# Two cross-attentions over a 6272-key context: a new share of tiles turned on TensorE, later masks and weights, shared channel bounds

## The chip, the core and the metric

The kernel runs on one core of a Trainium2 chip. A core has TensorE (matmuls, here PE), VectorE (DVE), ScalarE (ACT), GpSimd (POOL) and SyncE (SP), which here only issues DMAs. The metric is the time of one execution on the device in microseconds (us), the median of several runs.

## What is computed

Two layers of a small Perceiver work on 64 tokens of width 128. Each layer is a cross-attention over a context of 6272 keys, a second block (self-attention; in layer 1 a delta-rule block) and a feed-forward block. This text is about the two cross-attentions. Attention 0 has a mask over the keys, attention 1 has none.

```python
x = x + _L0_xattn_ref(_layernorm(x, axis=-1), ctx_1024, mask_SxS2_ik0, W_q, W_k, W_v, W_o)
...
x = x + _L1_xattn_ref(_layernorm(x, axis=-1), ctx_1024, Wq, Wk, Wv, Wo, bo)
# each: 16 heads of 64; softmax(q k^T / 8, masked to -1e20 in the first) v, then W_o
```

The kernel never forms keys and values. It folds W_k into the queries (the tile G, 128 channels by 1024 rows, a row for each head and token), takes scores as G times the transposed context, and multiplies the probabilities with the untransposed context. Each float32 operand is kept as two float16 parts, upper and lower, and three of their four products are summed.

## The kernel before

**Tiling.** The keys are cut into 7 chunks of 896 (CH, CK), the 1024 rows into 8 tiles of 128 (RT). An attention has STEPS = 56 steps, n = 8 c + r. Each step passes through every engine:

- TensorE: `score(n)`, six matmuls (L443); two steps ahead of everything else.
- VectorE: `maximum(n)` (L556) applies scale and mask, writes `probs` and the running maximum; `shifted` (L561).
- ScalarE: `exps(n)`: `alpha` (L499, one column) and the exponential of the tile (L502).
- Either by DMA: ScalarE makes the upper half in float16 (`upper`, L509), VectorE or GpSimd subtracts it (`lower`, L532), SyncE issues one transposing DMA for both halves (`turn`, L392) into `probsT`.
- Or on TensorE: `turn(n)` is seven transposes into PSUM banks 4 and 5 (L455), ScalarE copies out the upper part (L516, L518), VectorE subtracts for the lower (L589). The next turn waits for `p_lower`, that is, for those banks.
- TensorE: `pv(n)`, 21 matmuls (L475), five steps behind; VectorE adds to `den` and `U` (L569, L574), six steps behind.

`on_pe(L, n)` says which steps are turned on TensorE, `on_vector(L, n)` which lower parts VectorE makes; the rest is GpSimd's. Every engine works through its list in order. `maximum(n)` also waits until the lower part of step n - 4 is done (`probs` has four buffers). `halves` has five buffers, `probsT` four.

**Context and masks.** SyncE's queue loads the context chunks first (float32, into `moe`), with mask 0 behind chunk 2 and masks 1 and 2 at the end; the others and the weights are in its list at fixed steps (`MASK_AT`, `WEIGHTS_AT`). In attention 0 GpSimd scales each chunk (L1119), casts its upper part (L1120), subtracts for the lower (L1124) and makes the bfloat16 mask (L1113), two steps apart, from step 0 on: chunk 2 + n // 6. A second transposing DMA per chunk (`turn_ctx`, L382) makes the untransposed context `ctxN`.

**Scales.** Before the first scores VectorE takes the largest absolute value of each channel in each chunk (`channel_max_dve`, L612, seven times) and derives the scale of the context. TensorE sums squares over the channels (L709) for a bound of the scores, GpSimd takes the root (L666), and VectorE and ScalarE write G's upper and lower halves (L756, L765, L788). In `fold_q_pe` the first half of G's matmuls (L714) is ahead of L709 and the second behind it. `stay_warm` (L686) issues matmuls whose result nobody reads.

## Time and profile before

| | us |
|---|---|
| median of 3 runs | 465.6 (462.07 to 466.75) |
| the profiled execution | 461.98 |
| its span | 460.2 |

| engine | busy us | share |
|---|---|---|
| TensorE matmuls | 414.4 | 90% |
| VectorE | 346.8 | 75% |
| ScalarE | 280.7 | 61% |
| GpSimd | 226.3 | 49% |

Attention 0 lies between about 26 and 181 us of the span, attention 1 between about 228 and 374 us. "L443" is a line of the kernel. In the page each group of instructions has its count, busy time, mean duration and the idle time of its engine before it, with what ended that idle time. A row of the timeline gives the start and duration of an instruction or of a merged row of equal ones. All times are of this one execution.

### The profile page before, as it was taken

What the parts mean: (1) busy time and instruction counts of PE and PEld (TensorE: products, weight loads), DVE (VectorE), ACT (ScalarE), POOL (GpSimd) and SP (SyncE); (2) the same over time, 40 slices, a digit from 0 to 9 for tenths busy, and PEclk for the clock granted to TensorE, in tenths of its full rate; (3) what the DMA queues carried; (4) which work ended last, traced back from release to release, by engine and by line L of the source; (5) the groups of instructions that cost most, each with busy time, mean ns of one, the idle gap of its engine ahead of it and who ended that gap; (6) DMA issues with size and microseconds to landing.
All of it is one profiled execution on the core that took longest, in us unless ns stands there. A gap on an engine that the chain in (4) does not pass through costs nothing.

```text
span 460.2 us, 11503 instructions
## 1 busy us (share of the span) xinstructions
PE 414.4 (90%) x4488; PEld 331.4 (72%) x4488; DVE 346.8 (75%) x939; ACT 280.7 (61%) x549; POOL 226.3 (49%) x143
## 2 busy tenths in 40 slices
PE   6897999999999998999888998999999899974776
PEld 6865777777877787889656776777777689853675
DVE  3676888888778887456599989888888854488653
ACT  2148788878888882433297897988898611260210
POOL 1379888798556540010014698875566100169110
PEclk8578999999999999999999999999999999995979
DMA  8738999999998889900049999999999910000000
GB/s 292 234 41 161 228 208 269 226 229 199 153 187 150 154 130 335 374 1 5 1 80 196 172 190 184 185 180 201 191 193 195 180 31 1 1 0 1 1 0 3
DMA packets 191365, 66.33 MB, mean 144 GB/s; under 512 B 186752, under 2 KB 186960, under 8 KB 190544
## 3 DMA queue, kind: packets, MB, share of 16 engines
q1 hardware_dynamic: 191024, 64.56, 71.9%
q10 hardware_dynamic: 288, 1.05, 0.6%
q8 instruction: 35, 0.57, 0.5%
q14 instruction: 18, 0.15, 0.1%
HBM read 18.76 MB, written 0.03 MB: 41 GB/s over the span
## 4 chain that ended last, share of the span: by engine, by line
PE 45%; DVE 21%; DMA 9%; POOL 9%; ACT 7%; issue 6%; SPq 3%; DVEq 0%; ACTq 0%; POOLq 0%
PE ps L475 15%; PE ps L443 12%; DVE probs L556 8%; DMA probsT<-halves 7%; PE ps L686 6%; ACT probs L502 3%; DMA moe<-in_ctxT 3%; POOL halves L532 2%; PE ps L455 2%; ACT halves L509 2%; POOL moe L1196 2%; PE ps L930 2%; DVE U L574 1%; POOL moe L1191 1%; SPq L392 1%
## 5 line engine op out<-in xcount | busy, mean ns | idle before, releaser
L532 POOL TENSOR_TENSOR halves<-probs,halves 128x896 f16<-128x896 f32 x70 | 132.3, 1891 | 88.5 <-ACT halves L509 87.9
L443 PE MATMUL ps<-ctxT_parts,GT_parts 128*128 128x512 f16 (+1 forms) x672 | 147.8, 357 | 10.0 <-DVE negmax L556 9.2
L475 PE MATMUL ps<-ctxN,probsT 128*128 128x128 f16 x2352 | 148.4, 219 | 5.5 <-DMA probsT<-halves 4.9
L475 PEld LDWEIGHTS ps<-ctxN,probsT 128*128 128x128 f16 x2352 | 139.0, 98 | 19.7 <-issue 5.5
L502 ACT ACTIVATE probs<-probs,shifted 128x896 f32<-128x896 f32 x112 | 115.3, 1030 | 0.0
L443 PEld LDWEIGHTS ps<-ctxT_parts,GT_parts 128*128 128x128 f16 x672 | 61.4, 99 | 62.6 <-DVE negmax L556 12.8
L509 ACT CAST halves<-probs 128x896 f16<-128x896 f32 x95 | 87.6, 922 | 0.0
L556 DVE CUSTOM_DVE_ANT_0 probs<-ps,maskb,negmax 128x896 f32<-128x896 f32 x56 | 67.5, 1205 | 3.7 <-PE ps L443 3.7
L556 DVE CUSTOM_DVE_ANT_0 probs<-ps,zero,negmax 128x896 f32<-128x896 f32 x56 | 67.5, 1205 | 0.5 <-PE ps L443 0.5
L686 PE MATMUL ps<-cst 128*128 128x128 f32 x458 | 65.4, 293 | 0.0
L686 PEld LDWEIGHTS ps<-cst 128*128 128x128 f32 x458 | 60.5, 206 | 3.3 <-issue 2.1
L499 ACT ACTIVATE alpha<-negmax 128x1 f32<-128x1 f32 x112 | 32.9, 294 | 48.3 <-DVE negmax L556 47.4
L574 DVE SCALAR_TENSOR_TENSOR U<-U,alpha,ps 128x128 f32<-128x128 f32 x112 | 38.4, 343 | 31.0 <-PE ps L475 30.5
L681 POOL TENSOR_TENSOR rstd<-veps,cst 128x1 f32<-128x1 f32 x6 | 3.3, 556 | 76.7 <-DVE veps L672 76.7
L532 DVE TENSOR_TENSOR halves<-probs,halves 128x896 f16<-128x896 f32 x25 | 30.2, 1210 | 1.5 <-ACT halves L509 1.5
L569 DVE TENSOR_SCALAR den<-den,alpha,chunksum 128x1 f32<-128x1 f32 x112 | 30.2, 269 | 0.1
L1113 POOL TENSOR_SCALAR maskb<-moe 128x896 bf16<-128x896 int32 x6 | 19.3, 3217 | 5.6 <-DMA moe<-in_mask 5.2
L502 ACT ACTIVATION_READ_ACCUMULATOR probs<-probs,shifted 128x1 f32 x112 | 20.9, 187 | 0.0
L589 DVE TENSOR_TENSOR probsT<-ps,probsT 128x512 f16<-128x512 f32 (+1 forms) x34 | 19.5, 615 | 1.1 <-ACT probsT L516 1.1
L561 DVE TENSOR_SCALAR shifted<-negmax 128x1 f32<-128x1 f32 x112 | 17.2, 154 | 3.9
L455 PE MATMUL ps<-cst,probs 128*128 128x128 f32 x119 | 16.6, 282 | 1.2 <-DVE probsT L589 1.2
L1532 DVE SCALAR_TENSOR_TENSOR moe<-ps,moe 128x63 f32<-128x63 f32 (+62 forms) x63 | 15.8, 251 | 2.2
(344 smaller groups left out, 390.7 us busy)
## 6 DMA issues: line engine op xcount, KB each, us to landing
moe<-in_ctxT SPq DMA_DIRECT2D x7, 448.0 KB, 9.5
moe<-in_mask SPq DMA_DIRECT2D x12, 224.0 KB, 6.4
moe<-in_gateT SPq DMA_DIRECT2D x2, 1024.0 KB, 9.4
moe<-in_upT SPq DMA_DIRECT2D x2, 1024.0 KB, 10.9
moe<-in_downT SPq DMA_DIRECT2D x2, 1024.0 KB, 13.4
probsT<-halves SPq DMA_TRANSPOSE x95, 4.7
wv<-in_wv SPq DMA_DIRECT2D x2, 512.0 KB, 5.9
wo<-in_wo SPq DMA_DIRECT2D x2, 512.0 KB, 6.9
```

The source lines that it names most:

```text
L443: ins = pe.matmul(ps[:, 2 * b + h, 0:width], GT_parts[:, g_part, r * P:(r + 1) * P], ctxT_parts[:, keys:keys + width], start=(g_part == 0 ...
L455: ins = pe.transpose(ps[:, TURN_BANKS[t // 4], t % 4 * P:(t % 4 + 1) * P], probs[:, n % BUFS, t * P:(t + 1) * P], ident)
L475: ins = pe.matmul(ps[:, bank, 0:D], probsT_parts[:, b, p_part, k * P:(k + 1) * P], ctxN_parts[:, at:at + D], start=(p_part == 0 and c_part ...
L499: act.activation(alpha[:, n:n + 1], negmax[:, n:n + 1], ACT.Exp, bias=negmax[:, n + RT:n + RT + 1], scale=-1.0)
L502: act.activation(probs[:, n % BUFS, :], probs[:, n % BUFS, :], ACT.Exp, bias=shifted[:, n:n + 1], scale=-1.0, accum_out=chunksum[:, n:n + ...
L509: act.copy(halves_of(L, n)[:, 0, :], probs[:, n % BUFS, :]).then_inc(sem("upper_done"), 1)
L532: eng.tensor_tensor(halves_of(L, n)[:, 1, :], probs[:, n % BUFS, :], halves_of(L, n)[:, 0, :], ALU.subtract).then_inc(lower_of(L, n)[0], 1)
L556: dve.tensor_tensor_reduce(out=probs[:, n % BUFS, :], in0=scored, in1=added, scale=descale[:, L:L + 1], scalar=negmax[:, n:n + 1], op0=ALU ...
L569: dve.tensor_scalar(den[:, r:r + 1], den[:, r:r + 1], alpha[:, n:n + 1], chunksum[:, n:n + 1], ALU.mult, ALU.add).then_inc(sem("den_added" ...
L574: dve.scalar_tensor_tensor(U[:, r, :], U[:, r, :], alpha[:, n:n + 1], ps[:, PV_BANKS[n % len(PV_BANKS)], 0:D], ALU.mult, ALU.add).then_inc ...
L589: dve.tensor_tensor(probsT_parts[:, n % BUFS, 1, a:a + w], ps[:, TURN_BANKS[part], 0:w], probsT_parts[:, n % BUFS, 0, a:a + w], ALU.subtra ...
L686: pe.matmul(ps[:, bank, 0:P], ident, ident, start=True, stop=True)
```

## The change

- Masks: all behind the context in SyncE's queue, the last five behind the first `turn_ctx`; `par` with them. GpSimd makes mask 0 after the root of the bound, mask 1 at step 2, and prepares chunks 2 to 6 from step 4 (`POOL_FROM`).
- Weights: at steps 24 to 44 instead of 12 to 22.
- Channel bounds: ScalarE takes chunks 1 and 4 as sums of absolute values (`channel_sum_act`), VectorE the other five.
- G of attention 0: the two parities alternate, all before L709, with eight warming matmuls between; 12 instead of 4 warming matmuls before the scores. ScalarE's half of G waits for the scale alone. In attention 1 the second lower half of G is made behind `maximum(0)`.
- Turning: in both attentions the steps n % 8 == 5 and the last three are turned on TensorE (9 + 9), where attention 0 had n % 4 == 3 and the last two (15), attention 1 the last two (2). The last two turns use banks 0, 1 and 2, 3 and wait for no lower part.
- Lower parts: VectorE makes those of 0, 2, then n % 4 == 3 up to 27, and 52 in attention 0. Upper and lower part of step 0 are one place earlier in the lists of ScalarE and VectorE.
- `alpha` of the first eight steps is a constant 0, so their L499 goes. The scale keeps an even exponent.

```diff
+POOL_FROM = 4
...
-        MASK_AT = {1: 3, 4: 4, 7: 5, 10: 6}
-        WEIGHTS_AT = {2: ("par", par[:], "par"), 12: ("in1", w_qT, "wqT1"), 13: ("in1", wkT[:], "wkT1"),
...
+        WEIGHTS_AT = {24: ("in1", w_qT, "wqT1"), 27: ("in1", wkT[:], "wkT1"), 30: ("out0", wv[:], "wv0"),
+                      33: ("out0", wo[:], "wo0"), 36: ("ffn", win[:], "win"), 38: ("ffn", wout[:], "wout"),
+                      40: ("small_attn", a_w[:], "a_w"), 42: ("delta", d_w[:], "d_w"), 44: ("delta", w1s[:], "w1s")}
         def on_pe(L, n):
-            return L == 0 and n % 4 == 3 or n >= STEPS - 2
+            return n % 8 == 5 or n >= STEPS - 3
         def on_vector(L, n):
             if L == 0:
-                return n < 30 and n % 4 == 1 or n == STEPS - 3
-            return n % 4 == 3 or n in (0, 1, STEPS - 3)
+                return n in (0, 2) or 4 <= n < 30 and n % 4 == 3 or n == STEPS - 4
+            return n % 4 == 3 or n in (0, 1, STEPS - 4)
+        def turn_banks(n):
+            return {STEPS - 2: (0, 1), STEPS - 1: (2, 3)}.get(n, TURN_BANKS)
...
-                if c == 2:
-                    load_mask(0)
+            load_mask(0)
             load_mask(1)
-            load_mask(2)
+            load("par", par[:], "par")
             turn_ctx(0)
+            for c in range(2, CH):
+                load_mask(c)
...
-                if k > 0:
+                if k > 0 and n < STEPS - 2:
                     pe.wait_ge(sem("p_lower"), 2 * k)
...
-                if 1 <= i <= STEPS and not on_pe(L, i - 1):
+                if i == 0:
+                    upper(0)
+                if 2 <= i <= STEPS and not on_pe(L, i - 1):
                     upper(i - 1)
...
-                if 2 <= i < STEPS + 2 and on_vector(L, i - 2) and not on_pe(L, i - 2):
+                if i == 1:
+                    lower(dve, L, 0)
+                if 3 <= i < STEPS + 2 and on_vector(L, i - 2) and not on_pe(L, i - 2):
                     lower(dve, L, i - 2)
...
+                for j in range(PAIRS):
+                    for par_ in range(2):
+                        rows = slice(par_ * DK, (par_ + 1) * DK)
+                        ins = pe.matmul(ps[:, 4 + par_, j * S:(j + 1) * S], wkT[rows, j, :], QT[rows, j, :],
+                                        start=True, stop=True)
+                ins.then_inc(sem("g_ready"), 2)
+                stay_warm(pe, 6, 8)
+                pe.wait_ge(sem("squares"), 2)
+                pe.matmul(ps[:, 7, 2 * D:2 * D + 3], C("ones"), squares[:, 0:3], start=True,
+                          stop=True).then_inc(sem("bound_summed"), 1)
+                return
...
-                channel_max_dve(dve, range(0, 3))
+                channel_max_dve(dve, (0, 2))
...
-                channel_max_dve(dve, range(3, CH))
+                channel_max_dve(dve, (3, 5, 6))
...
+        def channel_sum_act(act, c):
+            act.wait_ge(sem(f"ld_ctxT{c}"), 16)
+            act.activation(probs[:, c // 4, :], ctxT_raw[:, c * CK:(c + 1) * CK], ACT.Abs,
+                           accum_out=ch_amax[:, c:c + 1]).then_inc(sem("ch_max"), 1)
...
-            stay_warm(pe, 6, 4)
+            stay_warm(pe, 6, 12)
...
+            bound_pool(pool, 0)
             mask(0)
-            bound_pool(pool, 0)
...
-            mask(1)
             for n in range(STEPS):
                 if not on_pe(0, n) and not on_vector(0, n):
                     lower(pool, 0, n)
-                c, part = 2 + n // 6, n % 6
-                if c < CH:
+                if n == 2:
+                    mask(1)
+                c, part = 2 + (n - POOL_FROM) // 6, (n - POOL_FROM) % 6
+                if n >= POOL_FROM and c < CH:
...
-            flash_dve(dve, 1, {2: keep_o1, 4: partial(weight_max, 0, win), 6: partial(weight_max, 1, wout),
+            flash_dve(dve, 1, {0: partial(g_lower_dve, dve, 1, 1), 2: keep_o1, 4: partial(weight_max, 0, win), 6: partial(weight_max, 1, wout),
```

## Rows read from the trace of the kernel before

**Rows 1.** The page: the chain that ended last, shares by engine.
```profile
PE 45%; DVE 21%; DMA 9%; POOL 9%; ACT 7%; issue 6%; SPq 3%; DVEq 0%; ACTq 0%; POOLq 0%
```

**Rows 2.** By stretch: busy PE, PEld, DVE, ACT, POOL; clock, DMA share, GB/s.
```profile
44.00:110.00 66.00, 63.76 (x722) 48.74 (x720) 56.41 (x143) 53.24 (x105) 56.35 (x30) 1.00 1.15 228
110.00:168.00 58.00, 57.77 (x665) 45.25 (x663) 47.83 (x127) 49.01 (x98) 33.10 (x18) 1.00 0.95 165
168.00:182.00 14.00, 12.17 (x190) 11.47 (x187) 12.40 (x43) 5.87 (x13) 1.69 (x1) 1.00 0.95 239
228.00:254.00 26.00, 22.76 (x197) 15.20 (x195) 24.66 (x54) 20.38 (x39) 7.72 (x5) 1.00 0.70 124
275.00:305.00 30.00, 28.08 (x316) 20.42 (x314) 27.86 (x68) 24.98 (x48) 25.70 (x15) 1.00 1.11 176
```

**Rows 3.** Chain in order of time (start us, us, what), both attentions.
```profile
144.03 1.14 PE ps L443 x6
145.93 1.17 PE ps L475 x21
...
266.09 1.14 PE ps L443 x6
...
268.40 1.14 PE ps L443 x6
```

**Rows 4.** Chain before the first scores; last, the timeline at 187 us.
```profile
18.16 1.10 DVE ch_amax L612
...
20.85 3.60 PE ps L714 x16
24.45 2.00 PE ps L686 x8
26.46 2.25 PE ps L443 x6
...
187.26 2.06 PE L727 MATMUL ps<-wkT,wq 64*128 64x128 f32 x32
```

**Rows 5.** By stretch, 174:188; waits at 275:374 (us, times, longest); SyncE's queue, attention 1.
```profile
174.00:188.00 14.00, 12.44 (x178) 11.44 (x176) 9.00 (x32) 2.24 (x4) 0.00 (x0) 1.00 1.03 371
...
PE ps L475 <- DMA probsT<-halves: 3.7, 8, 1.1
...
235.28 132.57 SPq L392 DMA_TRANSPOSE probsT<-halves  x54
```

**Rows 6.** Timeline: start us, us, instruction; VectorE's subtraction beside GpSimd's work.
```profile
35.61 1.68 POOL L1119 TENSOR_TENSOR moe<-moe,ch_scale 128x896 f32<-128x896 f32 x1
...
35.76 2.48 DVE L532 TENSOR_TENSOR halves<-probs,halves 128x896 f16<-128x896 f32 x1 [1.20 <-ACT halves L509]
...
44.98 3.22 POOL L1113 TENSOR_SCALAR maskb<-moe 128x896 bf16<-128x896 int32 x1
...
47.55 1.08 DVE L532 TENSOR_TENSOR halves<-probs,halves 128x896 f16<-128x896 f32 x1
```

**Rows 7.** Timeline: GpSimd at steps 4 and 34, and the first product.
```profile
43.01 1.89 POOL L532 TENSOR_TENSOR halves<-probs,halves 128x896 f16<-128x896 f32 x1 [0.16 <-ACT halves L509]
...
44.59 1.33 PE L475 MATMUL ps<-ctxN,probsT 128*128 128x128 f16 x21
...
123.72 1.89 POOL L532 TENSOR_TENSOR halves<-probs,halves 128x896 f16<-128x896 f32 x1 [0.94 <-ACT halves L509]
```

**Rows 8.** GpSimd's groups at 44:110: busy us, mean ns; idle before, its end.
```profile
L532 POOL TENSOR_TENSOR halves<-probs,halves 128x896 f16<-128x896 f32 x13 | 24.6, 1891 | 9.1 <-ACT halves L509 8.8
...
L1124 POOL TENSOR_TENSOR ctxT_parts<-moe,ctxT_parts 128x896 f16<-128x896 f32 x4 | 7.6, 1892 | 0.0
...
L1120 POOL CAST ctxT_parts<-moe 128x896 f16<-128x896 f32 x4 | 5.3, 1337 | 0.3
```

**Rows 9.** Timeline of the last turn of attention 0; the page's group of L589.
```profile
175.63 0.95 PE L455 MATMUL ps<-cst,probs 128*128 128x128 f32 x7 [1.18 <-DVE probsT L589]
...
L589 DVE TENSOR_TENSOR probsT<-ps,probsT 128x512 f16<-128x512 f32 (+1 forms) x34 | 19.5, 615 | 1.1 <-ACT probsT L516 1.1
```

More of the change, by code:

```diff
@@ L50 @@
 HALF_SCALE = 2.0 ** 15
-CTX_SCALE = 2.0 ** 14
+CTX_SCALE = 2.0 ** 13
+EVEN_EXPONENT = 0x7F000000
 PROB_SCALE = 2.0 ** 11
@@ L411, in _ @@
                     load(name, t, src)
-                if n == 22:
-                    load("delta", w1s[:], "w1s")
             sp.wait_ge(sem("ctxT_ready"), CH)
@@ L497, in exps @@
             def exps(n):
-                act.wait_ge(sem("negmax_ready"), base + n + 1)
-                act.activation(alpha[:, n:n + 1], negmax[:, n:n + 1], ACT.Exp, bias=negmax[:, n + RT:n + RT + 1],
-                               scale=-1.0)
+                if n >= RT:
+                    act.wait_ge(sem("negmax_ready"), base + n + 1)
+                    act.activation(alpha[:, n:n + 1], negmax[:, n:n + 1], ACT.Exp,
+                                   bias=negmax[:, n + RT:n + RT + 1], scale=-1.0)
                 act.wait_ge(sem("shifted"), base + n + 1)
@@ L588, in turned_lower @@
                     dve.wait_ge(sem("p_upper"), 2 * pe_index(L, n) + part + 1)
-                    dve.tensor_tensor(probsT_parts[:, n % BUFS, 1, a:a + w], ps[:, TURN_BANKS[part], 0:w],
+                    dve.tensor_tensor(probsT_parts[:, n % BUFS, 1, a:a + w], ps[:, turn_banks(n)[part], 0:w],
                                       probsT_parts[:, n % BUFS, 0, a:a + w], ALU.subtract).then_inc(sem("p_lower"), 1)
@@ L620, in channel_scales_dve @@
             seq(dve.tensor_reduce(whole, ch_amax[:, 0:CH + 1], AX, ALU.max))
-            seq(dve.tensor_scalar(whole.bitcast(I32), whole.bitcast(I32), 0x7F800000, None, ALU.bitwise_and))
+            seq(dve.tensor_scalar(whole.bitcast(I32), whole.bitcast(I32), EVEN_EXPONENT, None, ALU.bitwise_and))
             dve.tensor_scalar(u_back[:], whole, 1.0 / CTX_SCALE, None, ALU.mult)
@@ L704, in fold_q_pe @@
                 pe.wait_ge(sem("q_copied"), 2)
-            for par_ in range(2):
-                rows = slice(par_ * DK, (par_ + 1) * DK)
-                if i == 0 and par_ == 1:
-                    pe.wait_ge(sem("squares"), 2)
-                    pe.matmul(ps[:, 7, 2 * D:2 * D + 3], C("ones"), squares[:, 0:3], start=True,
-                              stop=True).then_inc(sem("bound_summed"), 1)
-                for j in range(PAIRS):
-                    out = ps[:, 4 + par_, j * S:(j + 1) * S]
-                    if i == 0:
-                        ins = pe.matmul(out, wkT[rows, j, :], QT[rows, j, :], start=True, stop=True)
-                    else:
-                        for side in range(2):
-                            rows = slice(side * S, (side + 1) * S)
-                            ins = pe.matmul(ps[rows, 4 + par_, j * S:(j + 1) * S], w_qk[par_][:, j, rows], src[:, 0:S],
-                                            start=True, stop=True)
+                for j in range(PAIRS):
[9 more added lines that the diff above has]
+                return
+            for par_ in range(2):
+                for j in range(PAIRS):
+                    for side in range(2):
+                        rows = slice(side * S, (side + 1) * S)
+                        ins = pe.matmul(ps[rows, 4 + par_, j * S:(j + 1) * S], w_qk[par_][:, j, rows], src[:, 0:S],
+                                        start=True, stop=True)
                 ins.then_inc(sem("g_ready"), 1)
@@ L748, in fold_q_dve @@
                 ctxT_first_dve(dve, 0)
+                ctxT_first_dve(dve, 1)
             if i < 2:
@@ L757, in fold_q_dve, with g_lower_dve @@
                               ALU.mult).then_inc(sem("g_scaled"), 1)
+            dve.wait_ge(sem("g_scaled"), i + 1)
+            g_lower_dve(dve, i, 0)
+            descale_dve(dve, seq, i, kappa)
             if i == 0:
-                ctxT_first_dve(dve, 1)
-            dve.wait_ge(sem("g_scaled"), i + 1)
-            for half in range(2):
-                if half == 1:
-                    dve.wait_ge(sem("g_upper"), i + 1)
-                cols = slice(half * 4 * P, (half + 1) * 4 * P)
-                dve.scalar_tensor_tensor(GT_parts[:, 1, cols], ps[:, 4 + half, :], g_scale[:, i:i + 1],
-                                         GT_parts[:, 0, cols], ALU.mult, ALU.subtract).then_inc(sem("g_copied"), 1)
-            descale_dve(dve, seq, i, kappa)
+                g_lower_dve(dve, i, 1)
+        def g_lower_dve(dve, i, half):
+            if half == 1:
+                dve.wait_ge(sem("g_upper"), i + 1)
+            cols = slice(half * 4 * P, (half + 1) * 4 * P)
+            dve.scalar_tensor_tensor(GT_parts[:, 1, cols], ps[:, 4 + half, :], g_scale[:, i:i + 1],
+                                     GT_parts[:, 0, cols], ALU.mult, ALU.subtract).then_inc(sem("g_copied"), 1)
+        def channel_sum_act(act, c):
+            act.wait_ge(sem(f"ld_ctxT{c}"), 16)
+            act.activation(probs[:, c // 4, :], ctxT_raw[:, c * CK:(c + 1) * CK], ACT.Abs,
+                           accum_out=ch_amax[:, c:c + 1]).then_inc(sem("ch_max"), 1)
         def fold_q_act(act, i):
@@ L773, in fold_q_act @@
                                accum_out=squares[:, 0:1])
+                channel_sum_act(act, 1)
                 act.wait_ge(sem("q_ready"), 1)
@@ L1098, in pseq @@
                 pool.wait_ge(sem("pool_step"), steps[0])
+            pool.memset(alpha[:, 0:RT], 0.0)
             pool.memset(den[:], 0.0).then_inc(sem("cleared"), 1)
```

17 lines of the change are left out of this document (8 added, 9 removed).

## The prediction

> **What bounds the kernel now.** I read the chain of work that ended last, then busy time by stretch, then single steps. Both attentions run 56 steps of one shape: scores, maximum, exponential, a float16 upper part by ScalarE and the rest (lower part) by VectorE or GpSimd, the turn of the tile by a DMA or on TensorE, and the product with the context. Almost half of the chain is TensorE [rows 1]. In the second half of attention 0 TensorE is busy for 57.8 of 58 us [rows 2]. There a step is 1.14 us of scores and 1.17 us of product, 2.31 us. After a turned tile there is a hole of 0.76 us between the two (144.03 + 1.14 = 145.17, and the next product is at 145.93) [rows 3]. So a tile turned on TensorE costs it 0.76 us, and with every fourth tile turned a step costs 2.50 us. Attention 1, with two turned tiles in all, runs at 2.31 us a step where nothing else holds it (266.09 to 268.40) [rows 3]. With every eighth tile turned a step would cost 2.31 + 0.76/8 = 2.40 us.
>
> Other limits are close. At 44 to 110, the first half of attention 0, GpSimd is busy 56.4 of 66 us. VectorE is busy 24.7 of 26 us at the start of attention 1, and 27.9 of 30 at 275 to 305. TensorE is idle for 2.2 us at 44 to 110. The DMA share is 1.15 with masks and weights among the tiles, and 0.95 without [rows 2].
>
> **Attention 0, start.** The masks now come behind the context, so 448 KB less lies before the last context chunk, which is waited for until 18.16 [rows 4]. At 371 GB/s [rows 5] that is 1.2 us. Two of the seven channel bounds go to ScalarE, idle then. That saves at most the 1.1 us of one bound [rows 4]. Against it, TensorE must now finish all matmuls of G and eight warming ones before the matmul of the bound. One parity of G takes 3.6 us at the low clock. With the parities alternating, as in L727, 32 such matmuls took 2.06 us at full clock [rows 4]. At half the clock I estimate 3.7 to 4.1 us for all 32, about what one half took before. They then end at about 18.7 us. Warming at 0.25 us an instruction (8 took 2.00 [rows 4]) adds up to 4 us, so the bound is summed at 22.1 to 22.9, against 20.85. Behind it come the square root on GpSimd, the scale and the G tile, about 4 us, while 24 more warming instructions run. The first scores then start at about 27 us against 26.46. But six matmuls of scores took 2.25 us at the low clock [rows 4] and take 1.14 at the full one, so the first maximum starts 0 to 0.9 us sooner. If the clock stays low, the scores start at 28 us or later and it is 1 to 2 us later.
>
> Then the first lower part moves to VectorE, directly behind step 1, instead of waiting behind GpSimd's context work. The subtraction of step 1, which took VectorE 2.48 us [rows 6], goes to GpSimd. Walking through the queues with these durations I get the maximum of step 4 at about 35.5 us and the first product at about 42 us, against 44.59 [rows 7]. Gain 2.5 us, range 0 to 4. GpSimd, however, has the mask of chunk 1 (3.22 us [rows 6]) in between, and I find it at step 4's lower part at 43.3 us, against 43.01 [rows 7].
>
> **Attention 0, steps 4 to 33.** This is what I think decides. GpSimd prepares five chunks there, each 1.68 and 3.22 us [rows 6] and 1.34 and 1.89 us [rows 8], with gaps 8.3. Of the 30 steps TensorE turns four (5, 13, 21, 29) and VectorE subtracts six, so 20 lower parts of 1.89 us, with gaps 1.93, stay for GpSimd. That is 41.5 + 38.6 = 80.1 us of work, against 80.7 us in which the old kernel came from step 4 (43.01) to step 34 (123.72) [rows 7]. TensorE would like 30 x 2.40 = 72 us. So GpSimd becomes the bound, reaches step 34 when it did before, and the saved turns bring nothing in this stretch. Products still come earlier, because the subtraction had slack: 8.8 us of GpSimd's idle time was waiting for ScalarE [rows 8]. I keep 2.3 of the 2.5 us.
>
> One thing speaks against the change here. VectorE's subtraction took 2.48 us where GpSimd's product had begun just before it (35.61 to 37.29), 1.4 more than the 1.08 us it took inside GpSimd's mask operation [rows 6]. The Trainium skill, page SBUF — State Buffer, section SBUF: two separate sides, says that a VectorE operation with two inputs in SBUF and a GpSimd operation exclude each other for the whole instruction. The first pair of rows agrees with that, the second does not.
>
> **Attention 0, steps 34 to 52.** TensorE turns two tiles (37, 45) instead of five: -2.3 us. But the weights now load at steps 24 to 44. From step 24 to 43 the queue has 18 tiles and 3 context turns. The 54 transposes of attention 1 took 132.6 us from first to last issue [rows 5], 2.4 us each, and I take 2.35. That is 49.4 us, and 3.1 MB of weights at 371 GB/s are 8.4 us more: 57.8 us, for steps that TensorE does in 48. From the issue of step 24 at about 96 us it ends at 154 to 156 us, where the old kernel was too. Some hides in the DMA's lead over the product; I charge 1.3 us. Sum -1.0, between -2.3 and +2.
>
> **End of attention 0.** Three tiles are turned on TensorE, the last two into score banks that are free. Before, the last turn waited 1.18 us for VectorE [rows 9]. TensorE is idle for 1.8 us at 168 to 182 [rows 2]; one turn more costs 0.76: -1.1 us. Attention 0 in all: -2.3 - 1.0 - 1.1 = -4.4 us, range -10 to +2.
>
> **Attention 1.** The new order puts the lower part of step 0 between maximum 1 and 2 on VectorE, where it waits for ScalarE's cast. Queued behind that wait are maximum 2 and, for its result, ScalarE's next exponential and the cast of step 1. G's second half (L765) moves behind maximum 0. I get maximum 4 one us later. Through step 9 the turned tile of step 5 adds VectorE's two subtractions (2 x 0.615 us [rows 9]) and a later place for each maximum, where VectorE has nothing to spare: +3.0 us, range +1 to +3.5. Six more turns (13 to 53) at 0.76 us cost +4.6, since TensorE is the bound there. In return 3.7 us of waits for DMA go [rows 5], because a tile in eight leaves the queue, and the last turn's wait of 1.2 us: -4.9. Sum +2.7, range -2 to +7. Between and behind the attentions nothing changes that lies on the path; G's ScalarE half no longer waits for VectorE's, worth 0 to 0.4.
>
> **Sum.** -4.4 + 2.7 = -1.7 us. The profiled execution took 461.98 us with a span of 460.2, and lies 3.6 below the median of 465.6. I move the difference onto the median: 463.9, forecast 464.0 us.
>
> **Rivals.** (A) As summed: GpSimd and the queue take back what TensorE gives in attention 0, and attention 1 loses a little: 464.0, own range 461 to 469.
> (B) Faster: GpSimd does not hold the pace, since 9.1 us of its time at 44 to 110 was idle [rows 8] and steps can shift against each other. Then six turns fewer count in full, -4.6, the 2.2 us idle at 44 to 110 go, and with the start's 2.5 and the end's 1.8 attention 0 gives 11; attention 1 at +1 makes 455.6. Against it: 80 us of work in 72.
> (C) Slower: in attention 1 the DMA turns were hidden, and only 1.2 of the 4.9 us comes back. Then it is +3.0 + 4.6 - 1.2 = +6.4 there, and slower over all by more than 1% once attention 0 gives less than 1.7 us. With half of my 4.4 it is 469.8.
> (D) Slower: the two engines exclude each other. Each of the six VectorE subtractions costs GpSimd 1.08 us while it is the bound, +6.5: 470.4. The mask operation, which excluded nothing, speaks against the full price. This is the rule of the Trainium skill, page SBUF — State Buffer, section SBUF: two separate sides, taken at its word.
>
> **Chances.** A 0.42, B 0.36 (TensorE's pace is the one limit that is certain), C 0.12, D 0.10. One per cent, 4.7 us, is about what a measurement of this kernel can tell from no change. A lies within it, B on the fast side, C and D at or beyond the slow edge: faster 0.36, same 0.42, slower 0.22. The range takes in B, C and D: 455.5 to 470.5.
>
> **What would show it.** A: GpSimd busy over 90% from step 4 to step 34, its waits for ScalarE gone; B: still over 5 us of them, and steps of 2.40 us from the start. Steps 44 to 52 of attention 0 at 2.40 us. First product near 42 us. In attention 1 the first product one us later behind the first scores than now, waits for DMA under 1 us, steps of 2.40. Attention 0 shorter by 3 to 6 us, attention 1 longer by 1 to 4. The forecast would be wrong if attention 1 gets shorter, or if GpSimd idles at 44 to 110 us as it did.

## The result, and the profile after

| | before | after |
|---|---|---|
| median | 463.93 us (462.07 to 466.75) | 472.87 us (472.15 to 475.42) |
| ratio, 95% interval | | 1.0219 (1.0169 to 1.0269) |
| span of the profiled execution | 460.2 us | 470.5 us |

The changed kernel is 2.2% slower, where 464.0 us was forecast. The forecast was set on 465.6 us, the median of three executions; with the fourth it is 463.93, and taken from there the forecast change of -1.7 us gives 462.2. I cut both spans at the first matmul of scores and the end of the last product of each attention:

| us | first scores at | attention 0 | between | attention 1 | rest |
|---|---|---|---|---|---|
| before | 26.25 | 155.03 | 46.58 | 145.96 | 86.37 |
| after | 26.56 | 159.47 | 46.58 | 152.93 | 84.92 |
| difference | +0.3 | +4.4 | 0 | +7.0 | -1.5 |

The rest holds the same work in all kernels of this study, and varies between 84.9 and 87.9 us with the moments at which the granted clock is low. The loss lies in the attentions. The span came out 12.0 us above the forecast change; attention 0 accounts for 8.8 of them (-4.4 forecast, +4.4 measured) and attention 1 for 4.3 (+2.7 and +7.0).

Busy time by stretch, after (columns as in [rows 2]):

```profile
44.00:110.00 66.00, 61.27 (x699) 46.49 (x697) 56.58 (x136) 51.98 (x102) 64.01 (x33) 1.00 1.06 180
110.00:126.00 16.00, 11.83 (x107) 8.53 (x105) 8.28 (x22) 9.93 (x21) 15.55 (x9) 0.79 1.12 222
126.00:168.00 42.00, 40.74 (x472) 31.08 (x470) 32.56 (x86) 34.59 (x67) 26.47 (x14) 1.00 1.10 208
```

GpSimd is busy 64.0 of 66 us at 44 to 110, 97%, against 56.4 in [rows 2]: the forecast's first mark. But the loss is not there. It is in the second line: TensorE is busy 11.8 of 16 us and the mean of its granted clock is 0.79. This is the chain of work there, in order of time (start us, us, what):

```profile
104.56 3.94 POOL maskb L1136
...
108.58 1.89 POOL halves L537
110.48 1.64 POOL moe L1142
...
113.38 6.78 DMA probsT<-halves
120.16 0.14 issue
120.29 2.40 PE ps L477 x21
122.69 2.24 PE ps L445 x6
124.93 1.67 PE ps L477 x21
```

The product at 120.29 is that of step 28. Its turn was issued at 113.38 and took 6.8 us to land, against a median of 4.5 on the page. The chain goes from the turn back into GpSimd's list, and this is misleading. The lower part of step 28 is the one that began at 108.58, behind the mask, and it was ready at 110.47. The one that the chain puts before the turn began at 113.19, ended at 115.08 and is step 30's, so it can't have released a turn issued at 113.38. SyncE's queue (timeline) shows what held the turn for 2.9 us: three turns, the context turn of the next chunk and a 512 KB weight at its new place, issued almost without a pause:

```profile
102.65 7.40 SPq L397 DMA_TRANSPOSE probsT<-halves  x3
110.10 2.14 SPq L387 DMA_TRANSPOSE ctxN<-ctxT_parts  x1
112.28 0.58 SPq L366 DMA_DIRECT2D wkT<-in_wkT  x1
113.38 6.27 SPq L397 DMA_TRANSPOSE probsT<-halves  x2
```

The weight took 6.3 us to land. The product of step 28 waited 4.2 us, and everything behind it waited too: VectorE issues in order, so the addition of this product (L579) stood in front of the maximum of step 35 (L561). VectorE, timeline:

```profile
115.32 1.21 DVE L561 CUSTOM_DVE_ANT_0 probs<-ps,maskb,negmax 128x896 f32<-128x896 f32 x1
...
122.73 0.35 DVE L579 SCALAR_TENSOR_TENSOR U<-U,alpha,ps 128x128 f32<-128x128 f32 x1 [5.80 <-PE ps L477]
122.99 1.21 DVE L561 CUSTOM_DVE_ANT_0 probs<-ps,maskb,negmax 128x896 f32<-128x896 f32 x1
```

One late turn thus stops the scores, the exponentials and the next turns, and the lead is gone. TensorE paused from 116.1 to 120.29 us, and the granted clock was at its lower level (1.2 GHz) from 119.01 to 125.83. The 21 matmuls of the product took 2.40 us instead of 1.33, and the three groups from 120.29 on took 6.1 us, where 1.17, 1.14 and 1.17 us at the full clock make 3.5. So about 2.7 us of the loss at this place is the clock's. In all, products of attention 0 waited for DMA three times after 44 us, 7.3 us in sum, where it was 1.1 us in before. After:

```profile
PE ps L477 <- DMA probsT<-halves: 7.3, 3, 4.2
```

The table sets the starts of products against the first scores of the same attention, in us.

| product of step | 0 | 4 | 8 | 24 | 36 | 48 | 55 |
|---|---|---|---|---|---|---|---|
| attention 0, before | 18.35 | 28.34 | 38.74 | 81.45 | 111.83 | 141.81 | 153.69 |
| attention 0, after | 15.49 | 26.23 | 37.16 | 79.30 | 115.61 | 145.59 | 158.13 |
| attention 1, before | 14.09 | 24.91 | 34.59 | 73.82 | 102.79 | 131.80 | 144.62 |
| attention 1, after | 14.97 | 28.21 | 38.18 | 79.74 | 109.96 | 139.21 | 151.59 |

In attention 0, steps 24 to 36 take 36.3 us instead of 30.4: +5.9. In attention 1, 3.6 of the 7.0 us are lost by step 8 and 3.8 more from there to step 48, as much as five turned tiles of 0.76 us cost. The row of waits for DMA that stood in [rows 5] with 3.7 us has no counterpart in attention 1 after.

### The profile page after: what moved, and what is told of

Its sections match the earlier page's. It is cut to its first block, busy times and chain, and to the rows that moved or that the text cites. A ratio compares the mean times of both kernels' runs of the same rounds, so it can differ in the third digit from the quotient of the medians.

```text
span 470.5 us, 11565 instructions
## 1 busy us (share of the span) xinstructions
PE 415.5 (88%) x4527; PEld 332.3 (71%) x4527; DVE 347.5 (74%) x939; ACT 279.6 (59%) x538; POOL 225.7 (48%) x143
## 3 DMA queue, kind: packets, MB, share of 16 engines
q1 hardware_dynamic: 189200, 64.10, 69.7%
## 4 chain that ended last, share of the span: by engine, by line
PE 42%; DVE 20%; POOL 19%; issue 6%; ACT 6%; DMA 5%; SPq 1%; DVEq 0%; POOLq 0%; ACTq 0%
PE ps L477 13%; PE ps L445 10%; DVE probs L561 8%; POOL halves L537 7%; PE ps L695 6%; DMA probsT<-halves 4%; POOL maskb L1136 3%; ACT probs L505 2%; ACT halves L512 2%; PE ps L457 2%; POOL moe L1220 2%; PE ps L952 2%; POOL moe L1142 2%; POOL ctxT_parts L1147 1%; POOL moe L1215 1%
## 5 line engine op out<-in xcount | busy, mean ns | idle before, releaser
L537 POOL TENSOR_TENSOR halves<-probs,halves 128x896 f16<-128x896 f32 x69 | 130.2, 1891 | 92.2 <-ACT halves L512 91.2
L477 PE MATMUL ps<-ctxN,probsT 128*128 128x128 f16 x2352 | 151.0, 221 | 8.6 <-DMA probsT<-halves 7.3
L477 PEld LDWEIGHTS ps<-ctxN,probsT 128*128 128x128 f16 x2352 | 141.8, 99 | 22.2 <-issue 7.8
L561 DVE CUSTOM_DVE_ANT_0 probs<-ps,maskb,negmax 128x896 f32<-128x896 f32 x56 | 67.5, 1205 | 3.1 <-POOL halves L537 2.5
L561 DVE CUSTOM_DVE_ANT_0 probs<-ps,zero,negmax 128x896 f32<-128x896 f32 x56 | 67.5, 1205 | 1.9 <-PE ps L445 1.3
L695 PE MATMUL ps<-cst 128*128 128x128 f32 x490 | 67.8, 288 | 0.0
L695 PEld LDWEIGHTS ps<-cst 128*128 128x128 f32 x490 | 62.9, 202 | 3.3 <-issue 2.1
L579 DVE SCALAR_TENSOR_TENSOR U<-U,alpha,ps 128x128 f32<-128x128 f32 x112 | 38.3, 342 | 35.3 <-PE ps L477 34.7
L502 ACT ACTIVATE alpha<-negmax 128x1 f32<-128x1 f32 x96 | 28.2, 294 | 49.1 <-DVE negmax L561 48.4
L537 DVE TENSOR_TENSOR halves<-probs,halves 128x896 f16<-128x896 f32 x25 | 31.7, 1268 | 2.4 <-ACT halves L512 2.3
L594 DVE TENSOR_TENSOR probsT<-ps,probsT 128x512 f16<-128x512 f32 (+1 forms) x36 | 20.6, 615 | 2.8 <-ACT probsT L519 2.8
L1136 POOL TENSOR_SCALAR maskb<-moe 128x896 bf16<-128x896 int32 x6 | 20.8, 3471 | 0.5
## 6 DMA issues: line engine op xcount, KB each, us to landing
moe<-in_downT SPq DMA_DIRECT2D x2, 1024.0 KB, 12.8
```

The source lines that it names most:

```text
L477: ins = pe.matmul(ps[:, bank, 0:D], probsT_parts[:, b, p_part, k * P:(k + 1) * P], ctxN_parts[:, at:at + D], start=(p_part == 0 and c_part ...
L502: act.activation(alpha[:, n:n + 1], negmax[:, n:n + 1], ACT.Exp, bias=negmax[:, n + RT:n + RT + 1], scale=-1.0)
L537: eng.tensor_tensor(halves_of(L, n)[:, 1, :], probs[:, n % BUFS, :], halves_of(L, n)[:, 0, :], ALU.subtract).then_inc(lower_of(L, n)[0], 1)
L561: dve.tensor_tensor_reduce(out=probs[:, n % BUFS, :], in0=scored, in1=added, scale=descale[:, L:L + 1], scalar=negmax[:, n:n + 1], op0=ALU ...
L579: dve.scalar_tensor_tensor(U[:, r, :], U[:, r, :], alpha[:, n:n + 1], ps[:, PV_BANKS[n % len(PV_BANKS)], 0:D], ALU.mult, ALU.add).then_inc ...
L695: pe.matmul(ps[:, bank, 0:P], ident, ident, start=True, stop=True)
```

## Experiments

All lengths of attentions and steps below are of one profiled execution each. Two theories for attention 0. Q: SyncE's queue and DMA decide. Six tiles more go by DMA, weights stand among them, and a late turn stops everything. G, the forecast's mechanism: GpSimd decides. For attention 1 the question is whether the turned tiles do it.

### Move the weights earlier

```diff
-        WEIGHTS_AT = {24: ..., 27: ..., 30: ..., 33: ..., 36: ..., 38: ..., 40: ..., 42: ..., 44: ...}
+        WEIGHTS_AT = {12: ..., 13: ..., 15: ..., 16: ..., 18: ..., 19: ..., 21: ..., 22: ..., 23: ...}
```

> The changed kernel, with the weights loaded at steps 12 to 23 again instead of 24 to 44. Theory Q (the queue: in the changed kernel the transpose of step 28 landed at 120.16 us behind a 512 KB weight issued at 112.28, the product waited 4.2 us for it, VectorE's list stood behind the product and the clock was low until 125.8): without weights at steps 27 and 30 this stall goes, the changed kernel's 472.9 us fall by 3 to 6 us. Theory G (GpSimd is full from step 4 to 33, so lower parts and with them the transposes come late whatever else is in the queue): 0 to -1.5 us, a stall of similar size stays near step 28 to 35.

Measured: 469.15 us against 463.54, ratio 1.0136 (1.0068 to 1.0203), attention 0 157.65, 1.8 less than after. That is less than Q expected (3 to 6), and the wait of step 28's product shrank from 4.2 to 1.2 us, where G expected a stall of similar size. The stall moved with the weights. It opens at step 16, whose product waited 2.35 us, and steps 12 to 20 take 26.4 us instead of after's 21.1. Waits at 44 to 110 (us, times, longest):

```profile
PE ps L475 <- DMA probsT<-halves: 6.8, 6, 2.4
```

With every eighth tile on TensorE, the weights opened a stall in both places tried.

### Lighten GpSimd

```diff
+            pool.memset(maskb[:, 2 * CK:], 0.0)
...
             def mask(c):
+                w = CK if c < 2 else 8
-                pool.tensor_scalar(maskb[:, c * CK:(c + 1) * CK], mask_raw(c), 0.0, ...
+                pool.tensor_scalar(maskb[:, c * CK:c * CK + w], mask_raw(c)[:, 0:w], 0.0, ...
```

> The changed kernel, with GpSimd's mask operation for chunks 2 to 6 cut to 8 of 896 columns (the rest of the mask is zero, so most of the key mask of these chunks is left out of the computation). Takes 5 x 3.2 to 3.9 us of work from GpSimd between steps 8 and 32 and nothing else. Theory G: attention 0 returns towards TensorE's pace of 2.40 us a step and loses 6 to 10 us, GpSimd's waits for ScalarE grow by about 16 us. Theory Q: at most 2 us less, the wait of the product of step 28 for its transpose stays.

The masks of chunks 2 to 6 are then left out but for 8 columns each, so this kernel computes something else; it serves as a measurement of time alone.

Measured: 469.54 us against 463.54, ratio 1.0107 (1.0036 to 1.0177). The profiled execution is the slowest of four, with a span of 470.1; attention 0 is 160.95 us in it, against after's 159.47. GpSimd lost its load, the stall stayed:

```profile
44.00:110.00 66.00, 61.69 (x699) 46.49 (x698) 57.55 (x140) 54.59 (x108) 54.52 (x35) 1.00 1.06 186
110.00:126.00 16.00, 11.91 (x114) 8.63 (x112) 8.01 (x21) 8.74 (x17) 9.07 (x6) 0.79 1.10 214
```

GpSimd is busy 54.5 instead of 64.0 us and TensorE gains next to nothing (61.7 against 61.3); waits for DMA are 8.0 us. The chain of work at the stall:

```profile
102.72 1.90 POOL halves L537
...
106.59 2.08 SPq L387
...
108.72 0.58 SPq L366
...
109.82 6.66 DMA probsT<-halves
...
116.61 2.40 PE ps L477 x21
```

The lower part of step 28 was ready at 104.61 and its turn was issued at 109.82: it lay 5.2 us behind other turns, the context turn and the weight. With the weights where the change puts them, GpSimd's load is not what opens the stall. Against the first scores the product of step 36 came 0.8 us sooner than in after and that of step 48 0.3 us; from step 48 to 52, with the granted clock low from 175.97 to 179.38 us, it lost 1.8, and so its attention 0 is the longer one. G had expected 6 to 10 us. How much the relief gives in the median is less sure: two executions with a granted clock of 0.956 took 471.7 and 471.9 us, after at 0.960 to 0.964 took 472.2 to 475.4, and two at 0.98 took 466.5 and 467.4. Of those two there is no trace.

### More tiles on TensorE in attention 0

```diff
-            return n % 8 == 5 or n >= STEPS - 3
+            return n % 8 == 5 or L == 0 and n % 4 == 1 and n > 1 or n >= STEPS - 3
```

> The changed kernel, with n % 4 == 1 (5, 9, 13, ... 49) and the last three tiles of attention 0 turned on TensorE instead of n % 8 == 5; attention 1 as changed. Takes six lower parts of 1.9 us from GpSimd and six transposes from the queue, three of them before step 30, and adds six turns of 0.76 us to TensorE. Theory G or Q: attention 0 gets 3 to 6 us shorter. Theory T alone (TensorE's own work sets attention 0): 2 to 4.6 us longer.

Measured: 466.71 us, ratio 1.006 (1.0024 to 1.0096), attention 0 155.92, waits for DMA 1.2 us. Steps 24 to 36 take 31.8 us instead of 36.3. Turning six tiles on TensorE, which costs it 4.6 us, still makes attention 0 3.6 us shorter. The edit relieves the queue and GpSimd together and doesn't tell the two apart.

### Weights behind the last turn

```diff
-        WEIGHTS_AT = {24: ..., ..., 44: ...}
+        WEIGHTS_AT = {}
...
+            load("out0", ...); load("in1", ...); load("small_attn", ...)
             load_experts(0)
             load_experts(1)
+            load("ffn", ...); load("delta", ...)
```

> The changed kernel, but none of the nine weight loads stands among attention 0's steps: all are issued behind its last turn, in the order in which they are needed (the values' and output weights, the folded ones, the small attention's, then the experts, the feed-forward's and the delta branch's). Theory Q (the transfers of turned tiles, context turns and 512 KB weights share one queue, and a weight ahead of a turn is what opens the stall of steps 28 to 36): that stall goes, DMA waits of attention 0 fall from 7.3 us to about 1, attention 0 falls from 159.5 to about 155.5 us, and the span by about 4 us, if the later weights are still in time for the gap between the attentions; if the gap pays, it shows as more than 46.6 us between the last product of attention 0 and the first scores of attention 1. Rival (the queue is full by its turns alone, 1.2 turned tiles and context turns more per eight steps than before): the stall moves but stays, attention 0 at 158 to 160 us.

Measured: 466.21 us, ratio 1.0072 (1.0038 to 1.0106). Attention 0 is 155.35 us, -4.1, as theory Q says; the stretch between the attentions grew by 0.4 us. Without the weights in the queue, the turn of step 28 was issued 1.8 us earlier against the first scores, at 110.48, and still took 6.1 us to land. Its product waited 1.6 us instead of 4.2, and the clock didn't fall there: the 2.7 us that this had cost are part of the 4.1. But waits for DMA are 4.4 us, not 1: a second limit shows behind the first. The chain of work from 99.71 to 124.87 us lies on GpSimd almost throughout. GpSimd at steps 32 to 34, timeline:

```profile
117.66 1.91 POOL L544 TENSOR_TENSOR halves<-probs,halves 128x896 f16<-128x896 f32 x1
119.66 3.22 POOL L1143 TENSOR_SCALAR maskb<-UT 128x896 bf16<-128x896 int32 x1
122.95 3.73 POOL L544 TENSOR_TENSOR halves<-probs,halves 128x896 f16<-128x896 f32 x2
```

The last mask stands between two lower parts. ScalarE had cast the upper part of step 33 from 117.00 to 117.92; GpSimd began its lower part five microseconds later.

### Both

> The kernel weights_end, and with GpSimd's mask operation cut to 8 of 896 columns in chunks 2 to 6 (the rest of the key mask of these chunks is left out of the computation). GpSimd gets about 3 us less work per chunk, 15 us in all over steps 4 to 33. If GpSimd bounds steps 4 to 33 once the queue is free (the prediction's term), attention 0 falls by 2 to 5 us below weights_end; if it does not, the two differ by less than 1 us.

This kernel, too, leaves out most of the masks. Measured: attention 0 151.56 us, 3.8 less than weights_end (median 462.90 against 466.21 on the same chip). Steps 24 to 36 take 31.2 us against 33.8. Busy time by stretch:

```profile
44.00:110.00 66.00, 61.82 (x701) 46.75 (x700) 56.81 (x137) 52.48 (x102) 54.87 (x35) 1.00 1.03 178
110.00:126.00 16.00, 14.52 (x166) 10.78 (x165) 12.39 (x34) 13.45 (x27) 13.34 (x9) 1.00 1.11 187
```

TensorE is busy 14.5 of 16 us in the second stretch, 13.3 in weights_end and 11.9 in light_masks. So GpSimd does bound, worth 3.8 us, once the weights are out of the queue. While they are in it, the same relief gave under 1 us up to step 48. The 3.8 us come behind step 24: up to it the two kernels differ by 0.6 us.

### The eighth pattern in attention 0 alone

The kernel before with

```diff
-            return L == 0 and n % 4 == 3 or n >= STEPS - 2
+            return L == 0 and n % 8 == 5 or n >= STEPS - 2
...
-                return n < 30 and n % 4 == 1 or n == STEPS - 3
+                return n < 30 and n % 4 == 3 or n == STEPS - 3
```

> The kernel before with one part alone: in attention 0 TensorE turns the steps with n mod 8 = 5 and the last two instead of every fourth, so that seven tiles more go by DMA there (and VectorE's lower parts move from the steps with n mod 4 = 1 to those with n mod 4 = 3). Weights at 12 to 23. Theory Q: the six or seven more turns fill the queue, the weights of steps 12 to 23 then open a stall as in early_weights, DMA waits of attention 0 go from 1 to 6 to 10 us and attention 0 gets longer, to 157 to 160 us although TensorE saves 7 times 0.76 = 5.3 us of transposes; ratio 1.005 to 1.01. Rival (the prediction's: fewer turned tiles are worth 2.3 us or nothing, the queue costs 1.3): attention 0 at 153.5 to 155.5 us.

Measured: 469.50 us, ratio 1.0141 (1.0063 to 1.0218). Attention 0 is 162.76 us, +7.7, more than either theory said, although TensorE turns six tiles less:

```profile
PE ps L475 <- DMA probsT<-halves: 11.4, 8, 2.5
```

Before puts masks and weights among the turns of steps 1 to 22. Steps 4 to 8 take 12.1 us (before 10.4) and steps 12 to 20 25.9 us (before 21.9). The edit also gives GpSimd eight lower parts more (40 instead of 32). This is not what held the turns: at seven of the eight waits the lower part was ready 3.1 to 7.8 us before SyncE issued its turn (step 12: ready 67.61, issued 75.36).

### The late weights alone

The kernel before with WEIGHTS_AT at 24 to 44.

> The kernel before with one part of the change alone: the nine weights at steps 24 to 44 instead of 12 to 23. In before the queue has 14 tiles less of attention 0 to turn, and its DMA waits in attention 0 were 1.1 us. Theory Q in its full form (a weight hurts only a queue that the turns already fill): attention 0 stays at 155.0 us within 0.7, ratio 1.00. Rival (a late weight by itself, next to the context turn and an odd-numbered row of turns, opens the stall): attention 0 at 157 to 159 us.

Measured: 461.82 us, ratio 0.9996 (0.9953 to 1.0038): no change in the time. Attention 0 is 157.89 us in its profile, which is the rival's figure and not Q's. But by the product of step 8 it is already 1.9 us behind before, and up to step 12 the two have the same code. The product of step 5 had waited 2.1 us for its turn, and the clock was low behind that. At step 24 it is still 1.9 us behind, and from 24 to 52 it takes 69.7 us against 68.7. A late weight costs little where every fourth tile is turned on TensorE.

This run also shows how much one execution can differ from another of the same code. TensorE, timeline:

```profile
38.78 1.31 PE L439 MATMUL ps<-ctxT_parts,GT_parts 128*128 128x512 f16 x6 [2.70 <-DVE negmax L552]
39.93 0.93 PE L451 MATMUL ps<-cst,probs 128*128 128x128 f32 x7
...
42.27 1.33 PE L471 MATMUL ps<-ctxN,probsT 128*128 128x128 f16 x21
```

The first product comes 16.47 us after the first scores (at 25.81), in before 18.35. In before the granted clock was at the lower level from 39.62 to 43.03 us, and the same groups took 2.27 and 1.68 us:

```profile
39.43 2.27 PE L443 MATMUL ps<-ctxT_parts,GT_parts 128*128 128x512 f16 x6 [2.71 <-DVE negmax L556]
41.49 1.68 PE L455 MATMUL ps<-cst,probs 128*128 128x128 f32 x7
```

In b_weights_late the low stretch came at 58.46 to 61.87 instead.

### The start alone

The changed kernel with the tiles, the weights' steps and attention 1's order of before.

> The part of the change that concerns the start, alone: masks behind the context, channel bounds shared with ScalarE, the reordered first weights, the earlier first products, the three more steps before GpSimd begins to prepare context; but TensorE turns the tiles that it turned before (attention 0 every fourth and the last two of both), VectorE's lower parts are those of before, the nine weights stand at steps 12 to 23 as before, and attention 1's step 0 has its order of before. The start of the first product is 2.8 us earlier against the first scores. If attention 0's queue and GpSimd leave room for it (14 tiles on TensorE instead of 8), it is kept: attention 0 at 152 to 153 us, attention 1 at 146.0, ratio 0.993 to 0.995. If the start gain is eaten whatever the tiles are, because GpSimd or VectorE now gets its context work later, attention 0 is at 154.5 to 156 us and the ratio is 1.00.

Measured: 460.69 us (455.27 to 463.90), ratio 0.9888 (0.9757 to 1.002): probably faster, not settled by its interval. Attention 0 is 153.63 us, 1.4 less than before, and its first product comes 15.98 us after the scores, 0.5 sooner than the 16.47 of b_weights_late, in which the clock was not low there.

### Attention 1 without its turned tiles, and with them alone

```diff
-            return n % 8 == 5 or n >= STEPS - 3
+            return L == 0 and n % 8 == 5 or n >= STEPS - 3
```

> The changed kernel, with only the last three tiles of attention 1 turned on TensorE (no n % 8 == 5 there); attention 0 as changed. Theory T (in attention 1 TensorE and VectorE are the bounds, each turned tile costs TensorE 0.76 us and VectorE 1.2 us, and the DMA queue had room): attention 1, 152.9 us from first scores to last product, gets 4 to 6 us shorter. Theory R (the queue was the bound and the turned tiles pay for themselves): 0 to 1.5 us shorter, waits for DMA grow from under 1 to 4 us or more.

> The kernel before with one part of the change alone: in attention 1 every step with n mod 8 = 5 is turned on TensorE (seven tiles), the other parts of the change left out. Theory T (a turned tile costs TensorE its transposes and the waits around them, and the DMA turns that it replaces were hidden): attention 1 goes from 146.0 to about 152 us, DMA waits there to about 0, ratio 1.012 to 1.015. Rival (the loss in attention 1 needs the other parts, such as the order of step 0 or three tiles at the end): under 148 us and a ratio under 1.005.

Measured: l1_by_dma has 463.27 us, ratio 0.998 (0.9939 to 1.0022). Its profiled execution took 469.68 us, with a low clock between the attentions (211.15 to 217.97 us) and not in attention 1. Attention 1 is 145.56 us, 7.4 less than after, with all of this in its waits for DMA:

```profile
PE ps L477 <- DMA probsT<-halves: 1.1, 5, 0.3
```

b_l1turn (the kernel before with n % 8 == 5 turned in attention 1) has 467.44 us, ratio 1.011 (1.0059 to 1.0161), and attention 1 is 152.42, 6.5 more than before. Taking the tiles out and putting them in give nearly the same. Five tiles from step 8 to 48 cost 3.7 us in b_l1turn and 3.8 in after. The tile of step 5 costs 2.7 us in both. There the clock has a low stretch too, from 258.95 to 262.37 us in after. After, TensorE:

```profile
258.76 2.27 PE L445 MATMUL ps<-ctxT_parts,GT_parts 128*128 128x512 f16 x6 [2.06 <-DVE negmax L561]
260.82 2.08 PE L477 MATMUL ps<-ctxN,probsT 128*128 128x128 f16 x21
```

In weights_end, whose attention 1 has the same code and no low stretch there, these two groups took 1.31 and 1.34 us, the tile of step 5 cost 1.5 us, and attention 1 took 151.69.

Where did the waits for DMA go? TensorE's waits from the product of step 8 to that of step 48 in attention 1, before (262.45:359.6) and after (270.8:371.8):

```profile
PE ps L443 <- DVE negmax L556: 1.6, 4, 0.9
PE ps L475 <- DMA probsT<-halves: 1.1, 3, 0.4
...
PE ps L445 <- DVE negmax L561: 3.2, 9, 0.9
```

Of before's 3.7 us of waits for DMA only 1.1 lay in these 40 steps, 2.7 in the last seven. After has none, but TensorE waits 1.6 us more for VectorE's maxima.

### Versions that beat both kernels

best: weights behind the last turn, l1_by_dma, and attention 1's step 0 in its order of before. best_quarter: that, and n % 4 == 1 turned on TensorE in attention 0 from step 5 on.

> The changed kernel with three edits: the weights behind attention 0's last turn as in weights_end; attention 1 turns no tile on TensorE but its last three; and step 0's upper and lower part in attention 1 come at their place of before. Attention 1: theory says 145.0 us (145.6 without its eight turned tiles, and its first product 0.9 us earlier, of which some two thirds last), against 145.96 before. Attention 0: as weights_end, about 155.5. Span 460.2 - 0.5 + 0.5 - the rest of the start: about 459 to 461; ratio to before 0.99 to 1.00. If the queue's stall stays, attention 0 is at 159 us and the ratio is 1.00 to 1.005.

> The kernel best (weights behind attention 0's last turn, attention 1 without turned tiles but the last three, its step 0 as before), and in attention 0 TensorE turns every step with n mod 4 = 1 from step 5 on, six tiles more than best. These cost 6 times 0.76 = 4.6 us of TensorE and take 6 DMA turns and 6 lower parts of GpSimd or VectorE away. Theory (in best the stall of steps 32 to 37 is GpSimd's lower parts behind its mask operations, worth 2.9 to 3.8 us): the two about cancel, attention 0 at 154 to 156 us, ratio 0.990 to 0.995. If TensorE bounds steps 4 to 50 throughout, attention 0 is at 157 us or more.

Measured: best 458.36 us against 463.39, ratio 0.9919 (0.988 to 0.9958), attentions 155.05 and 145.81. best_quarter 458.62 against 462.60, ratio 0.9899 (0.9865 to 0.9934), attentions 154.56 and 145.01. Both beat before by about 1%. The six extra tiles on TensorE cost nothing net, as expected, and in best_quarter the waits at 44 to 185 us have no row for DMA any more (2.6 us in best).

The lengths of attention 0 in one table, by where the weights stand (us). The rows differ in which tiles TensorE turns, the columns share the start of the change. start_only has also VectorE's steps and the last two tiles of before.

| | steps 12 to 23 | steps 24 to 44 | behind the last turn |
|---|---|---|---|
| every fourth tile | 153.6 (start_only) | 155.9 (l0_quarter) | 154.6 (best_quarter) |
| every eighth tile | 157.7 (early_weights) | 159.5 (after) | 155.4 (weights_end) |

Every eighth instead of every fourth costs 4.0 and 3.6 us with weights among the turns, and 0.8 without. Where two kernels have the same code in attention 0, their lengths lie 0.3 to 1.2 us apart (best and weights_end; after and l1_by_dma, 159.96; before and b_l1turn, 156.22), up to step 8 even 1.9. So 0.8 is no difference and 4 is one. The rows differ in GpSimd's load too, by six lower parts, so the table alone doesn't tell the queue from GpSimd.

## Why the prediction was wrong, step by step

**First scores, first product.** Forecast about 27 and about 42 us; measured 26.56 and 42.06. VectorE's first lower part took 1.77 us, the maximum of step 4 came at 36.02 (35.5). The walk was right, the gain was not: it was taken against 44.59 in [rows 7], and of those 2.9 us about 1.9 were the low clock of before's one execution, as b_weights_late shows. A reading of the clock in before beside the product would have told it.

**Steps 4 to 33.** GpSimd at 97% and its idle time gone: right. To step 24 the lead fell from 2.9 to 2.2 us, although TensorE had turned three tiles less (2.3 us): the saved turns brought nothing there, as said. The reason given for it, that GpSimd bounds, is borne out in small part only. Steps 8 to 24 took 42.1 us, where TensorE alone would need 38.4 (16 x 2.40), and still 41.5 in light_masks, where GpSimd has idle time again. TensorE waited there for VectorE's maxima, 2.6 us in after and 2.0 in light_masks. The figure was right in part by luck. And the stretch ended with a stall of 5.9 us in steps 24 to 36 that the sum did not have. The failing step is the queue's. I counted 57.8 us of queue work for 48 us at steps 24 to 43 and charged 1.3 us, because "some hides in the DMA's lead over the product". That treats a full queue as a rate. What decided was one turn, which was issued 2.9 us after its lower part was ready and landed 6.8 us later, behind a context turn and a weight. VectorE's order carried the wait of the product into the maxima, and the clock fell in the pause. weights_end puts 4.1 us on the weights. weights_end_light puts 3.8 us on GpSimd's load behind them. The two don't add with the late weights in place: light_masks alone gave under 1 us up to step 48.

A second reading in that term was wrong. "It ends at 154 to 156 us, where the old kernel was too" is not what the trace of before has. There SyncE issued the turn of step 44 at 149.73 us (timeline of SyncE, before and then after):

```profile
149.73 24.25 SPq L392 DMA_TRANSPOSE probsT<-halves  x8
...
158.71 1.55 SPq L397 DMA_TRANSPOSE probsT<-halves  x1
```

So the count itself said that the queue would fall 5 to 7 us behind before, and it did: after issued the turn of step 43 at 153.64 us and that of step 44 at 158.71, 9 us later than before, and its product came 4.9 us later. The 2.35 us for a turn was also read from attention 1, where turns follow the loop's pace of one a step; at steps 24 to 43 of after their issues took 2.2 us each.

**Steps 34 to 52 and the end.** Forecast -1.0 and -1.1; from the product of step 36 to that of step 55 the measurement is 42.5 us against 41.9: +0.7. A further wait for DMA of 1.3 us stands before the product of step 44, behind another weight and context turn. One of 1.9 us stands before that of step 51; weights_end has it too (1.7), so it isn't the weights'. Its cause is open. The three last tiles on TensorE gave no gain that shows: steps 48 to 55 took 12.5 us, before 11.9, and 12.3 in best.

**Attention 1.** The front was right: first product 0.9 us later (forecast one), and 3.6 us lost by step 8 (forecast +3.0), of which 0.9 the order of step 0, and 2.7 step 5's tile. The price of a tile, 0.76 us, was right. The failing step here is the credit of 4.9 us. Waits for DMA went from 3.7 us to none and nearly nothing came back: from step 8 to 48 the loss is 3.8 us, the full price of five tiles. The 1.1 us of waits for DMA in these steps were replaced by waits for VectorE's maxima, which grew by 1.6. The waits of 2.7 us in the last seven steps and the bank wait's 1.2 us gave 0.4 together, with one tile more, that of step 53, turned on TensorE there (steps 48 to 55 take 12.4 us instead of 12.8). This is the mechanism of rival C and nearly its price: +3.0, +4.6 and -1.2 forecast, +3.6, +3.8 and -0.4 measured, in sum +6.4 and +7.0. C had 0.12.

**Rivals B and D.** B fell: TensorE did not run at its own pace at steps 4 to 33. D's mechanism is in the rows. Timeline of after, three places:

```profile
30.58 1.89 POOL L1147 TENSOR_TENSOR ctxT_parts<-moe,ctxT_parts 128x896 f16<-128x896 f32 x1
...
31.65 1.77 DVE L537 TENSOR_TENSOR halves<-probs,halves 128x896 f16<-128x896 f32 x1 [0.92 <-ACT halves L512]
...
72.12 3.22 POOL L1136 TENSOR_SCALAR maskb<-moe 128x896 bf16<-128x896 int32 x1
...
73.15 1.08 DVE L537 TENSOR_TENSOR halves<-probs,halves 128x896 f16<-128x896 f32 x1
...
104.21 1.22 DVE L537 TENSOR_TENSOR halves<-probs,halves 128x896 f16<-128x896 f32 x1
...
104.56 3.94 POOL L1136 TENSOR_SCALAR maskb<-moe 128x896 bf16<-128x896 int32 x1
```

VectorE's first lower part ended at 33.42, 0.95 us behind GpSimd's two-input operation (32.47). The 2.48 us of [rows 6] end at 38.24, again 0.95 behind the end of GpSimd's product at 37.29. The other way round, GpSimd's mask took 3.94 us instead of 3.22 where it began inside a subtraction. In after four GpSimd operations of steps 4 to 33 were lengthened like this, by 3.2 us in sum, half of D's 6.5; in before two were, by 1.6. But a subtraction that began inside a mask operation took its 1.08 us and lengthened nothing, in [rows 6] and at 73.15. The Trainium skill, page SBUF — State Buffer, section SBUF: two separate sides, has a VectorE operation with two inputs in SBUF and a GpSimd operation that reads SBUF exclude each other for the whole instruction. The first and the last pair agree with that, the subtraction inside the mask operation does not. What the exclusion costs the attention is not shown: no run varied VectorE's subtractions by themselves.

**The marks.** "The forecast would be wrong if attention 1 gets shorter, or if GpSimd idles": neither happened, and it was wrong all the same. Both marks tested the gains. None looked at the one term with work above capacity.

## What to carry to other kernels

Where a queue's planned work exceeds its time, don't charge the excess as an average: find the moment where a large load and an extra turn meet, and see what stands in order behind the consumer. Eight waits for DMA, 3.7 us in sum, are no credit for an edit that gives the same engine 0.76 us more to do at each tile: ask which wait comes next. Loads that nobody needs soon belong behind the last transfer whose latency counts: that was worth 4 us here, of which about 2.7 were the clock that fell in the pause. And a chain in a profile can name the wrong releaser where several operations share a semaphore: compare the end of the operation named with the start of what it is said to have released.

## What the runs showed that I had not expected

- The queue hid GpSimd's limit: relief of GpSimd was worth under 1 us up to step 48 with the weights in the queue and 3.8 us in the whole attention without (151.56 against 155.35).
- 512 KB of weights took 6.3 us from issue to landing among the turns, and the turn issued 1.1 us behind it 6.8 us instead of 4.5. Without the weight the same turn took 6.1 us.
- VectorE's subtraction ended 0.95 us behind the two-input operation of GpSimd beside which it began, in before and in after.
- The same code reached its first product 16.47 or 18.35 us after its first scores, depending on whether the granted clock was low at 39.62 to 43.03 us.
- The first scores of kernels with the same start came at 21.4 to 26.6 us. The granted clock was low until 23.43 us in after; in l0_quarter, the earliest, it was not low from 7.91 to 250.26 us.
